# Routing a mixture of experts in two sets of token tiles, with a fixed region per expert and a table of first rows

## The reference

```python
x = _layernorm(x + attention(x))            # RMS norm, q/k/v, causal softmax, gated heads, wo
logits = xf @ Wg                            # [2048, 16]
_, topi = jax.lax.top_k(logits, 2)
gates = jax.nn.softmax(jnp.where(mask, logits, -jnp.inf), axis=-1)
for e in range(16):
    h = jax.nn.silu(xf @ W1[e] + b1[e]) * (xf @ W11[e] + b11[e])      # 128 -> 256
    y = y + (h @ W2[e] + b2[e]) * gates[:, e, None]
z = jax.nn.silu(xf @ Ws1 + bs1) * (xf @ Ws11 + bs11) @ Ws2 + bs2      # 128 -> 512 -> 128
x = _layernorm(x + (y + z))
```

## Time and profile before

| what | us |
|---|---|
| median of 3 executions (lowest, highest) | 682.15 (680.07, 682.47) |
| the profiled execution, its own time | 682.44 |
| its span in the trace | 679.3 |
| busy in the span: PE, DVE, ACT, POOL | 619.2, 484.1, 418.7, 121.3 |
| attention ends (last addition into `x_acc`) | 510.97 |
| first slot cast, last scatter issued | 528.94, 572.63 |
| first expert product, last scatter of results issued | 577.78, 652.82 |

### The profile page before, as it was taken

The page is one execution under the profiler, slowest core; times in us unless marked ns, Lnnn a source line. Parts: engine busy times, 40 slices in busy tenths (PEclk is TensorE's granted clock), DMA queues, the critical chain, the costliest instruction groups (busy, mean ns, idle before and its releaser), DMA issues.

```text
span 679.3 us, 14812 instructions
## 1 busy us (share of the span) xinstructions
PE 619.2 (91%) x5300; PEld 509.4 (75%) x5300; DVE 484.1 (71%) x1564; ACT 418.7 (62%) x909; POOL 121.3 (18%) x243
## 2 busy tenths in 40 slices
PE   4899999999999999999999999999968898999930
PEld 2678888858888886888888688888856366999930
DVE  3788767688877677877767797776788533668736
ACT  4786556687666568765656877556664211677746
POOL 4000000002000000000000000000000676688830
PEclk9899999999999999999999999999987899899985
DMA  6520000050000005000000498000067211333242
GB/s 139 118 55 1 1 2 1 2 125 1 1 2 1 1 2 116 10 1 1 3 1 1 94 194 27 1 1 2 1 200 175 37 48 55 83 90 89 79 127 85
DMA packets 56504, 33.57 MB, mean 49 GB/s; under 512 B 23920, under 2 KB 49776, under 8 KB 56432
## 3 DMA queue, kind: packets, MB, share of 16 engines
q1 hardware_dynamic: 53872, 27.38, 19.5%
q0 software_dynamic: 2560, 5.26, 2.3%
HBM read 14.75 MB, written 9.48 MB: 36 GB/s over the span
## 4 chain that ended last, share of the span: by engine, by line
PE 68%; DVE 10%; POOL 10%; issue 6%; DMA 2%; ACT 2%; SPq 1%; DVEq 0%; POOLq 0%; ACTq 0%
PE ps_o L1079 19%; PE ps_t L966 18%; PE ps_s L1048 12%; PE ps_s L1050 10%; POOL x_sorted L466 5%; PE ps_o L1089 4%; POOL y_rows L482 4%; DVE k_l L672 3%; DVE q_hl L672 2%; PE ps_s L1199 2%; POOL row_all L473 1%; PE ps_s L974 1%; ACT k_h L501 1%; PE ps_o L1187 1%; DVE bn L707 1%
## 5 line engine op out<-in xcount | busy, mean ns | idle before, releaser
L966 PE MATMUL ps_t<-ident,probs 128*128 128x128 f32 x1104 | 173.7, 275 | 12.0 <-ACT probs L513 11.9
L966 PEld LDWEIGHTS ps_t<-ident,probs 128*128 128x128 f32 x1104 | 135.1, 141 | 48.8 <-issue 11.6
L544 ACT ACTIVATE probs<-probs,nmax 128x128 f32<-128x128 f32 (+15 forms) x128 | 153.6, 1200 | 21.2 <-DVE nmax L775 12.3
L784 DVE COPY probsT<-ps_t 128x512 f32<-128x512 f32 (+3 forms) x160 | 91.2, 570 | 101.4 <-PE ps_t L966 100.4
L555 ACT ACTIVATE probsT<-ps_t 128x512 f32<-128x512 f32 (+3 forms) x160 | 89.6, 560 | 98.7 <-PE ps_t L966 97.3
L1048 PE MATMUL ps_s<-k_h,q_hl 128*128 128x512 f32 (+3 forms) x320 | 142.3, 448 | 0.5 <-DMA k_l<-k_l 0.5
L1079 PE MATMUL ps_o<-probsT,v_sb 128*64 128x128 f32 x2176 | 140.0, 277 | 1.3 <-DVE x_acc L799 1.2
L1079 PEld LDWEIGHTS ps_o<-probsT,v_sb 128*64 128x64 f32 x2176 | 116.8, 137 | 19.6 <-issue 14.6
L770 DVE TENSOR_SCALAR_CACHE_REDUCE probs<-ps_s 128x512 f32<-128x512 f32 x192 | 128.4, 686 | 0.7
L1050 PE MATMUL ps_s<-k_l,q_hl 128*128 128x512 f32 (+3 forms) x320 | 117.0, 366 | 0.0
L438 POOL TENSOR_TENSOR rden<-rsum,gate 128x2 f32<-128x2 f32 x64 | 12.5, 195 | 402.6 <-ACT probs L544 387.4
(11 more groups left out here) (148 smaller groups left out, 706.2 us busy)
## 6 DMA issues: line engine op xcount, KB each, us to landing
k_h<-k_h SPq DMA_DIRECT2D x32, 128.0 KB, 2.3
k_l<-k_l SPq DMA_DIRECT2D x32, 128.0 KB, 2.4
w_all<-in_L_ffn_W SPq DMA_DIRECT2D x2, 2048.0 KB, 11.0
xg<-x_sorted SPq DMA_DIRECT2D x48, 64.5 KB
x_sorted<-zeros SPq DMA_DIRECT2D x12, 256.0 KB, 8.5
act_s<-y_rows SPq DMA_DIRECT2D x8, 256.0 KB, 4.8
x_acc<-in_L_attn_tokens SPq DMA_DIRECT2D x4, 256.0 KB, 3.8
out<-x_acc SPq DMA_DIRECT2D x4, 256.0 KB, 2.3
```

Source lines behind the costliest of these rows:

```text
L544: nc.scalar.activation(probs[s % 2][h][:, 0:w], probs[s % 2][h][:, 0:w], ACT.Exp, bias=nmax[:, row], scale=-1.0, accum_out=rsum[:, row]).t ...
L784: nc.vector.tensor_copy(probsT[s % 2][h][:, c * BT:c * BT + w // P, :].rearrange("p n i -> p (n i)"), ps_t[1][:, 0:w]).then_inc(moved1, 1)
L966: return nc.tensor.transpose(dst, src, ident[:, :])
```

## The change

It has six parts.

1. Each expert gets a fixed region of 2,048 rows in `x_sorted` (17 regions, the last for unused tiles), so an expert's first row no longer depends on the others' counts. Zeros now take 68 blocks and row numbers 17 DMAs; half of the zeros go ahead of the first pair's copies of keys, half behind them, the row numbers behind the second pair's.
2. Routing runs in two sets of eight tiles: set 0 is the chunks n0 and n1, set 1 the chunks n2 and n3. `largest_logits`, `choose`, `places`, `place`, `gates` run per set; the count of set 0 is carried into set 1. Pool's loop over the tiles waits per set, and keeps its cast ahead of each pair of scatters.
3. SP reads tile n from the row that a table gives (`row_i`, made by `rows_of_slots` on DVE), which it loads into registers eight at a time.
4. The norm's rstd is a power on Pool (`row_scale`) instead of a square root on ACT and a reciprocal on DVE. The end of the last pair has its units' order written out by hand.
5. Gates come from Tanh on ACT in place of Exp and a division; the turned gates of the two sets go over separately.
6. The work of routing is put between the blocks of the dense part: on DVE, PE and ACT by the block number n. The PSUM banks and the SBUF places change with it.

The diff, cut to its core:

```diff
-    units + [("turn_x", 0, 0, c, 0) for c in (n0, n1)] if last else units
+    PE:  ending(..., [t14a, wo12, pv13, t14b, t15a, wo13, t15b, pv14, pv15, unit("turn_x", c=n0), wo14, wo15,
+                      unit("turn_x", c=n1)])
+    ACT: ending(..., [wo12, pv13, t14b, t15a, wo13, pv14, t15b, wo14, pv15, wo15, unit("turn_x", c=n0),
+                      unit("turn_x", c=n1)])
+    DVE: ending(ahead(ahead(pair_units(True, DVE_LAG), unit("times_wo", 10), unit("stats", c=n0)),
+                      unit("times_wo", 11), unit("stats", c=n1)),
+                [wo12, unit("norm", c=n0), t14b, pv14, wo13, t15a, t15b, pv15, unit("norm", c=n1),
+                 unit("stats", c=n2), wo14, wo15])
...
 SP
+            empty_groups(range(groups // 2))
             for p in range(PAIRS - 1):
                 for x in PE_UNITS[0]:
                     if x[:2] == ("project", K):
                         k_across(...)
-            (12 blocks of zeros, one DMA of 6,144 row numbers)
+                if p == 0:
+                    empty_groups(range(groups // 2, groups))
+                if p == 1:
+                        for r in range(E + 1):
+                            sp.dma_start(numbers[r, :, :, D].bitcast(i32),
+                                         empty_row[:, r * REGION:(r + 1) * REGION]).then_inc(zfill, 16)
...
+            sp.wait_ge(table_ready, 1)
+            load_rows(0)
             sp.wait_ge(scattered, 16 * TOPK * NT)
             for n in range(SLOT_TILES):
+                if n % IDS == 1 and n // IDS + 1 < SLOT_TILES // IDS:
+                    load_rows(n // IDS + 1)
...
-                sp.dma_start(xg[:, n % XB, :], x_sorted[n * P:(n + 1) * P, :]).then_inc(xg_in[n % XB], 16)
+                at = first_rows[n // IDS % 2][n % IDS]
+                sp.dma_start(xg[:, n % XB, :], x_sorted[bass.ds(at, P), :]).then_inc(xg_in[n % XB], 16)
...
 Pool
+            def row_scale(i):
+                pool.wait_ge(var_ready, i + 1)
+                nc.gpsimd.tensor_tensor(rstd[:, 0, cols], rstd[:, 1, cols], halves[:, cols], ALU.pow).then_inc(ln_rstd, 1)
...
-            pool.wait_ge(rows_ready, NC)
-            pool.wait_ge(slots_ready, 1)
-            for t in range(NT):
+            for i, tiles in enumerate(SETS):
+                pool.wait_ge(rows_ready, 2 * (i + 1))
+                pool.wait_ge(slots_ready, i + 1)
+                for t in tiles:
                     (cast, wait, two scatters as before)
+                    if i == 0 and t == tiles[0]:
+                        row_scale(3)
...
 ACT
+            act.preload_act_table(ACT.Silu)
+            rows_twice(n0)
+            rows_twice(n1)
...
-            nc.scalar.activation(gat[:, 1, :], gat[:, 0, :], ACT.Exp).then_inc(gexp, 1)
             for n in range(NC * SB):
                 (Silu of block n)
+                if n == 1: gate_difference(0)      # Tanh of set 0
+                if n == 4: x_across(n2); rows_twice(n2)
+                if n == 5: x_across(n3); rows_twice(n3)
+                if n == 6: gates_across(0)
+                if n == 7: gate_difference(1)
+                if n == 13: gates_across(1)
...
 DVE
+            def place(i):
+                if i == 1:
+                    link(nc.vector.tensor_copy(counts[1][:, :, 0], before[0][:, :, HALF]))
+                dve.wait_ge(count_psum, i + 1)
+                link(nc.vector.tensor_copy(counts[i][:, :, 1:], ...))
+                link(nc.vector.tensor_tensor_scan(before[i], carry, counts[i], 0.0, ALU.mult, ALU.add))
+                link(nc.vector.tensor_tensor(rank[:, cols, :], bank, before[i], ALU.add))
+                link(nc.vector.tensor_tensor(picked[:, :, cols, :], hot[:, :, cols, :], rank, ALU.mult))
+                nc.vector.tensor_reduce(slot_f[:, :, cols], picked[:, :, cols, :], X, ALU.add).then_inc(slots_ready, 1)
...
-            (norm of n2 and n3, three calls of largest_logits, 13 operations from counts to slots)
+            largest_logits(0)
+            choose(0)
+            for n in range(NC * SB):
+                shared_act(n)
+                n == 0: place(0), stats n3     n == 2: norm n2      n == 3: norm n3      n == 4: gates(0)
+                n == 5: largest_logits(1)      n == 6: choose(1)    n == 7: place(1)     n == 8: shared_add(0)
+                n == 9: gates(1)               n == 10: tiles_of_experts()              n == 12: shared_add(1)
+                n == 13: experts_of_slots()    n == 14: rows_of_slots()
...
 PE
             norm("logits", n0)
             norm("logits", n1)
-            (turning and logits of n2 and n3; shared_up(0); counts of all 16 tiles)
+            shared_up(0)
+            pe.wait_ge(acc_done, ONE + PAIRS * NT)
+            shared_up(1)
+            places(0)
+            for n in range(2, NC * SB):
                 shared_up(n)
+                n == 4: turn_x n2       n == 5: turn_x n3, logits n2
+                n == 6: gates_across(0), logits n3         n == 13: gates_across(1)
...
             def shared_down(i):
+                pe.wait_ge(gT_ready, 1 if NORM_ORDER[i] in (n0, n1) else 2)
                 for j in range(BT):
+                    if i == 0 and j == 2:
+                        places(1)
```

More of the change, by code:

```diff
@@ L101, in pair_units @@
                 stages.append([("times_wo", s - 3, 0, 0, 0)])
-            if last:
-                stages.append([(stage, 0, 0, c, 0) for stage, c in norm_at.get(s, [])])
-            else:
+            if not last:
                 stages.append([("project", w, 0, c, 0) for w, c in project_at.get(s, [])])
@@ new lines, in unit, with ending, ahead @@
+    def unit(stage, s=0, h=0, c=0, w=0):
+        return stage, s, h, c, w
+    def ending(units, tail):
+        cut = units.index(unit("scores", NT - 1, 1, 0, 2 * P)) + 1
+        assert set(units[cut:]) <= set(tail) and not set(tail) & set(units[:cut])
+        return units[:cut] + tail
+    def ahead(units, after, x):
+        at = units.index(after) + 1
+        return units[:at] + [x] + units[at:]
+    START = [("project", w, 0, c, 0) for c in range(NC) for w in (K, Q)] + [("project", V, 0, c, 0) for c in range(NC)]
@@ L164, in attention_moe_layer @@
         it = sb("it", [1, SLOT_TILES, E], f32)
-        counts = sb("counts", [P, E * NT + 1], f32)
-        ones_row = sb("ones_row", [P, E * NT + 1], f32)
+        region = sb("region", [P, E], f32)
+        it1 = sb("it1", [1, SLOT_TILES], f32)
+        counts = [sb(f"counts{k}", [P, E, HALF + 1], f32) for k in range(2)]
+        ones_row = sb("ones_row", [P, E], f32)
+        carry = sb("carry", [P, E, HALF + 1], f32)
+        halves = sb("halves", [P, NT], f32)
         ones_b = sb("ones_b", [P, P], bf16)
@@ L205, in attention_moe_layer @@
         rank = sb("rank", [P, NT, E], f32, moe)
-        before = sb("before", [P, E * NT + 1], f32, moe)
+        before = [sb(f"before{k}", [P, E, HALF + 1], f32, moe) for k in range(2)]
         cnt_i = sb("cnt_i", [P, E], i32, moe)
@@ new lines, in _ @@
+            for n in range(NC * SB):
+                shared_act(n)
+                if n == 0:
+                    place(0)
+                    norm("stats", n3)
+                elif n == 2:
+                    norm("norm", n2)
+                elif n == 3:
+                    norm("norm", n3)
+                elif n == 4:
+                    gates(0)
+                elif n == 5:
+                    largest_logits(1)
+                elif n == 6:
+                    choose(1)
+                elif n == 7:
+                    place(1)
+                elif n == 8:
+                    shared_add(0)
+                elif n == 9:
+                    gates(1)
+                elif n == 10:
+                    tiles_of_experts()
+                elif n == 12:
+                    shared_add(1)
+                elif n == 13:
+                    experts_of_slots()
+                elif n == 14:
+                    rows_of_slots()
@@ L901, in _ @@
+            shared_add(NC - 2)
             shared_add(NC - 1)
@@ L1138, in shared_down, with places @@
                 mm.then_inc(down_s, 1)
+            def places(i):
+                tiles = SETS[i]
+                cols = slice(tiles[0] * E, (tiles[-1] + 1) * E)
+                pe.wait_ge(routed_ready, i + 1)
+                nc.tensor.matmul(count_bank(i)[:, 2 * P:3 * P], tri_b[:, :], routed[:, cols], start=True, stop=True)
+                nc.tensor.matmul(count_bank(i)[:, 3 * P:4 * P], ones_b[:, :], routed[:, cols],
+                                 start=True, stop=True).then_inc(count_psum, 1)
```

347 lines of the change are left out of this document (196 added, 151 removed).

## The result

| | before | after |
|---|---|---|
| median of 4 executions (lowest, highest), us | 682.31 (680.07, 684.03) | 667.68 (666.79, 668.74) |
| the profiled execution, its own time; its span | 682.44; 679.3 | 666.86; 664.9 |

The ratio is 0.9764, with a 95% interval of 0.9731 to 0.9797: 14.6 us faster. The prediction was 673.7 with a range of 669.5 to 678.5.

A forecast was written before the change was run, and what follows sets the result against it. Two chains were taken to end together: Pool's scatters and PE's dense part. The first expert product moves from 577.78 to 569.1 with what follows unchanged, so 682.44 - 8.7 = 673.7 us, range 669.5 to 678.5.

The forecast's parts named there:

- Step 1: End of attention: the new order of DVE, ACT and PE work ends the last addition at 507.5, 3.5 us earlier.
- Step 2: Last addition to first cast: eight tiles chosen alone, two dense blocks ahead of the counts; cast at 516.4, 12.5 us earlier.
- Step 3: Pool's scatter chain: 44.65 us plus 0.3 for powers and 2.9 for DVE's company; last scatter over at 564.3.
- the 6.8 us counted in full: Pool's scatter chain: by the skill's full-blocking rule the added DVE work counts in full, 3.9 us more than the sum.
- Step 4: Second set's slots: there at 535.7 at full clock or 538, wanted by Pool at 540; no wait, margin 2.
- Step 5: Reading by table: SP's load of eight first rows before its second read costs 0.65 us, bounds 0 and 1.3.
- Step 6: PE's dense part: 46.2 and 4.5 of work plus waits and half clock; ends at 567.0 instead of 573.92.
- Step 7: Filling the sorted buffer: zeros and row numbers fit SP's free time between copies of keys; cost 0.
- Rival A: Clock stays full and DVE's company costs Pool nothing: some 12 us off, 670; chance 0.14.
- B: Pool held up by DVE's work in full (3.9) or a late second set: 677.6, or 679 with both; chance 0.18.
- C: Row numbers dearer than bounded, third copy of keys queues behind them on SP: 686 and up; chance 0.05.
- D: DVE work in attention and the dense part takes from PE what the early start gives: 681 to 684; chance 0.07.

The follow-up runs named there:

- Experiment 1: Changed kernel with the old order at attention's end put back: DVE's alone 672.83 us, ratio 0.9834; DVE's, PE's and ACT's 676.95 us, ratio 0.9903.
- experiment 3: Changed kernel plus eight unused DVE operations of 0.93 us behind dense blocks 8 to 15: two inputs in SBUF 670.80 us, one input 667.74 us.
- The activation's edit: Changed kernel with DVE's activation of dense block 1 ahead of the last chunk's statistics: 668.72 us, ratio 0.9770.
- the three edits: Changed kernel with one cast a set, both register table loads ahead of the wait, block 1's activation before the last statistics: 665.07 us, ratio 0.9711.

## Why the prediction was wrong, step by step

The view of the bound (two chains that end together, Pool's scatters in front) was right, and so were the parts that it listed. Four sizes were off, nearly all to one side.

*Step 1, last addition 507.5; it was 505.83.* The walk of the new order gave 506.7, and 0.8 were put on top for the moved statistics. They cost less: from the last pair's first copy of keys to the first weight load on SP it is 117.21 us (381.01 to 498.22) against 116.91 before (381.59 to 498.50), so 0.3; with DVE's old order put back it is 116.92. So of the 1.7 too much, the term "their price, I take 0.8" makes 0.5. Another 0.6 is there before that stretch: the profiled execution after has the last pair's copies of keys at 381.01 instead of 381.59, 0.5 of it from the very first copies on (14.63 against 15.13). The last 0.6 lies in the walk (124.8 us from the last pair's copy to the addition instead of the walk's 125.1 plus 0.3); no row shows which of its steps. Experiment 1 shows that DVE's order is what brings this step.

*Step 2, from there 8.9 to the first cast; it was 7.08.* The failing term is "so I take the middle, 513.5", between dense blocks at full and at half clock. The text gave the reason for full clock itself (the denser tail) and then split the difference. The rows show 1.00 up to 516: the two blocks end 4.2 behind the last addition, as the full-clock case had it (511.7 against 507.5). Two cases with chances would have said more than their middle. Experiment 1 shows the other case, 5.75 us later, about 4.8 of it by the clock.

*Step 3, Pool's chain 47.9; it was 45.70.* Two terms. The power was "as small as the cast, 0.3"; it takes 1.05 for 128x4, so it was at the scatter's end of the bounds. Company was priced at 0.4 us for each us, which the eight operations of experiment 3 give too (0.42), and then multiplied with the wrong amount: the 9.4 us counted norms and small operations with one input, a kind that cost nothing in experiment 3. Work with two tensor inputs beside the chain is some 5.5 us (gates 1.6, choice 0.7, placing 1.3, two tables 1.86, from the timeline), and much of it starts while a scatter is already running, where it costs nothing either. The chain grew by 1.05, which the power alone makes: company grew by nothing, where the sum had 2.9. Behind the first tile, what single tiles take over 2.70 adds up to 0.74 before (one scatter, the 1.71) and to 0.74 after (five tiles, at most 0.30). That these are equal is chance, and so in part is the price: with DVE's old order (experiment 1) the same work starts inside other Pool instructions, one cast takes 0.94, and the chain is 46.73. The prediction's other reading, the 6.8 us counted in full, is out as well: a Pool instruction was held at most for what was left of an operation, and by one-input work not at all.

*Step 4, the second set in time: right.* Its slots were there at 533.45, before the 535.7 walked, and Pool wanted them at 536.53. The margin is 3.1 us. On the chips with stalls it is gone, a wait of 4.08.

*Step 5, the load of first rows 0.65: right within 0.3.* From the last scatter to the first product it is 5.15 against 4.19, 0.96 more. The load itself is 0.53, and 0.4 to 0.7 come back when the second load is taken off the path.

*Step 6, PE's chain to 567.0; it ended at 560.46.* From the first dense block at 506.34 that is 54.1, against the 50.7 of bare work (46.2 + 4.5) and 8.1 of added waits and half clock. The end is 6.5 early: 1.9 because the dense part starts earlier (step 1, nearly all), the rest in this sum. Two terms of it failed by about the same. "Half clock twice, 3.5": it came once and cost some 1.8 (the blocks at 515.82 and 517.35, and the dense part's end in the kernel of experiment 1 in which the clock stays up). The added waits, 2.6 and 2: PE's are 2.08 and 0.46. The bare work, 50.7, was some 0.9 too high as well. The activation's edit takes off 2.7, most of the wait and the fall of the clock. The Tanh cost no table load: ACT's only one in the stretch stands at 505.39, ahead of the first Silu, where before there were two, at 522.76 and 524.29.

*Step 7, filling hidden: right,* though the zeros were dearer than costed and the numbers cheaper. The halves of the zeros took 55.18 and 53.54 us of SP, 1.6 a block instead of 1.02, and the numbers 50.25 instead of at most 86 (SP's timeline, the answer to the earlier trace rows):

```profile
41.92 55.18 SPq L390 DMA_DIRECT2D x_sorted<-zeros  x34
149.65 53.54 SPq L390 DMA_DIRECT2D x_sorted<-zeros  x34
270.57 50.25 SPq L403 DMA_DIRECT2D x_sorted<-empty_row  x17
381.01 1.11 SPq L365 DMA_DIRECT2D k_h<-k_h  x2
```

The prediction's ground for "company costs nothing", 120.90 us from one step to its like, was no comparison, since the pair's length was taken from the same two steps. The rows before and after give one: from copy of keys to copy of keys it is 120.74 with zeros beside it (139.37 to 260.11) and 120.90 with the numbers (260.11 to 381.01), against 120.78 and 120.91 before, where no filling runs beside them (139.90, 260.68, 381.59).

Beyond the steps, 0.4 us went after the first product and 1.2 outside the span. The differences add up: -1.7 - 1.8 - 2.2 + 0.3 - 0.4 - 1.2 = -7.0, against 666.86 - 673.7 = -6.8.

Rival A, more off by full clock and by company at nothing, is what happened; it said 670 with a chance of 0.14. It stopped short by the earlier last addition (1.7) and the time outside the span (1.2), and left out that the power takes 0.75 more. The 1.2 outside the span isn't the change's: it differs by as much between executions of one kernel (last section). B, C and D are out: no hold of Pool beyond 0.5 us in the changed kernel, copies of keys on time, PE's end earlier and not the same. The range was too narrow on the low side because errors of steps 1, 2 and 3 were treated as bounds that lean to either side, while the reasons given in the text itself leaned to the fast one, but for the power.

## What to carry to other kernels

When work is split so that a serial engine can start on the first half, the second half may come later than it did unsplit; what counts is whether the serial engine is then still busy with the first. Price a clock that has two levels as two cases with chances, and not by the mean. In these traces the low level came behind pauses of PE, but the same pause of 2.08 us brought it in one kernel and not in another. Before a measured price of interference is multiplied, sort the work by kind: only operations of the kind that showed it, and of these only those that start first.

## What the hardware showed beyond that

- The granted clock costs about 4.8 us (an estimate from rows of experiment 1) when it is at 0.50 from the end of attention to the counts. It stays there though PE works without a pause from 508.02 to 519, while with DVE's order alone it is back within some 3.5 us.
- A power of 128x4 numbers on Pool takes 1.01 to 1.11 us, in four of four; a cast of two columns takes 0.20 where nothing holds it.
- Profiled executions fall in two groups by the second pair's copies of keys (139.1 to 139.9, or 141.1 to 142.1 us), the kernel with the three edits in both. The time outside the span is 1.7 to 2.0 or 3.0 to 3.1 us from one profiled execution to the next. Traces have to be compared from an event near the stretch in question.
- Chips differ more than these kernels: the kernel before takes 682 to 684 us in the first result and on chips 2, 4 and 6, and 703 and 713 on chips 9 and 11.
